# Cross-attention and int8-style FFN on one core: tokens laid out transposed outside the kernel, a levelled Wq, and another order on TensorE

## The reference

```python
def _attn_block(x, y):                       # x is layernorm(x)
    y_main, y_dca = y[:, :-16], y[:, -16:]
    kv_dca = y_dca @ Wkv_dca + bkv_dca       # keys and values of the 16 dca rows
    q = _ln(heads(x @ Wq + bq), qn_w, qn_b)  # 16 heads of 32, normalised per head
    k, v = ...                               # from y_main @ Wk + bk, y_main @ Wv + bv
    ctx = softmax(q k / sqrt(32)) v  +  softmax(q k_dca / sqrt(32)) v_dca
    return ctx @ Wo + bo
x = x + _attn_block(_layernorm(x), ctx_1024)
x = x + fake_quant(relu(fake_quant(_layernorm(x)) @ fake_quant(kernel) + bias))
```

## Time and profile before

| | |
|---|---|
| time, median of 3 runs | 368.29 us (367.71 to 371.18) |
| the profiled execution | 370.66 us, its span 368.8 us |
| PE busy | 319.3 us, 87% |
| DVE busy | 315.0 us, 85% |
| ACT busy | 222.5 us, 60% |
| POOL busy | 174.3 us, 47% |
| mean granted TensorE clock | 0.965 |

### The profile page before, as it was taken

One profiled execution on the slowest core, in us unless ns is written; L12 is line 12 of the kernel. 1 busy time (PEld: TensorE's weight loads), 2 busy tenths in 40 slices (PEclk: granted clock), 3 DMA queues, 4 the chain that ended last, 5 costly groups with the idle time before them and its releaser, 6 DMA issues.

```text
span 368.8 us, 7583 instructions
## 1 busy us (share of the span) xinstructions
PE 319.3 (87%) x2338; PEld 257.3 (70%) x2353; DVE 315.0 (85%) x804; ACT 222.5 (60%) x444; POOL 174.3 (47%) x261
## 2 busy tenths in 40 slices
PE   1498989799989999999898999999998999868732
PEld 0345657688877878787787888878787878566620
DVE  2987899799979899989898998989998999975664
ACT  3357886366666767676758585848584856552501
POOL 5201513327281828282828281828282837281620
PEclk9999899699999999999999999999999999998985
DMA  8870458507070909190909082828292616180002
GB/s 267 263 265 1 82 121 142 125 29 163 15 177 11 194 22 191 34 199 18 195 17 189 31 139 81 128 93 130 92 135 84 123 54 123 54 145 2 28 0 85
DMA packets 36451, 39.14 MB, mean 106 GB/s; under 512 B 8760, under 2 KB 27452, under 8 KB 36412
## 3 DMA queue, kind: packets, MB, share of 16 engines
q1 hardware_dynamic: 36044, 38.40, 48.2%
q10 hardware_dynamic: 368, 0.27, 0.3%
HBM read 17.15 MB, written 4.72 MB: 59 GB/s over the span
## 4 chain that ended last, share of the span: by engine, by line
PE 52%; DMA 9%; SPq 7%; issue 7%; DVE 3%; ACT 2%; POOL 0%; ACTq 0%; DVEq 0%
PE bank L1323 26%; SPq L372 7%; PE bank L1440 7%; DMA q_stack<-q_lo 7%; PE bank L1409 4%; PE bank L1596 4%; PE bank L1606 2%; PE bank L1420 2%; PE bank L1421 2%; PE bank L1463 2%; PE bank L1493 1%; DMA k_stack<-k_lo 1%; ACT k_hi L606 1%; PE bank L1498 1%; PE bank L1455 1%
## 5 line engine op out<-in xcount | busy, mean ns | idle before, releaser
L1440 PE MATMUL bank<-v_aug,prob_store 128*128 128x66 f32 x512 | 68.6, 278 | 3.4 <-ACT prob_store L744 3.4
L511 POOL TENSOR_TENSOR k_lo<-wkv_raw,k_hi 128x448 f16<-128x448 f32 x16 | 16.7, 1042 | 113.8 <-issue 105.9
L1440 PEld LDWEIGHTS bank<-v_aug,prob_store 128*128 128x128 f32 x512 | 64.4, 195 | 5.9 <-ACT prob_store L744 4.6
L1056 DVE TENSOR_REDUCE neg_max<-bank 128x4 f32<-128x448 f32 (+1 forms) x128 | 45.2, 416 | 9.9 <-PE bank L1409 9.9
L755 ACT ACTIVATE wkv_raw<-bank,affine 128x448 f32<-128x448 f32 (+1 forms) x32 | 22.4, 747 | 42.4 <-PE bank L1493 42.1
L744 ACT ACTIVATE prob_store<-bank,exp_scale 128x512 f32<-128x512 f32 x64 | 41.6, 677 | 4.9 <-PE bank L1421 4.8
L530 POOL TENSOR_TENSOR finals<-seg_out 128x128 f32<-128x128 f32 x64 | 34.4, 546 | 13.7 <-DVE seg_out L1069 13.4
L1420 PE MATMUL bank<-q_stack,k_stack 128*128 128x128 f16 x256 | 33.9, 220 | 1.9 <-ACT maxT L606 1.9
L1421 PE MATMUL bank<-maxT,sel 128*128 128x128 bf16 x256 | 33.7, 219 | 0.0
L1420 PEld LDWEIGHTS bank<-q_stack,k_stack 128*128 128x128 f16 x256 | 26.4, 104 | 6.1 <-issue 3.9
L1069 DVE TENSOR_TENSOR seg_out<-bank,rden 128x256 f32<-128x256 f32 x64 | 27.2, 424 | 3.8 <-POOL finals L530 1.7
(11 more groups left out here) (213 smaller groups left out, 876.9 us busy)
## 6 DMA issues: line engine op xcount, KB each, us to landing
x_in<-in_x SPq DMA_DIRECT2D x16, 256.0 KB, 4.9
q_stack<-q_hi SPq DMA_DIRECT2D x32, 128.0 KB, 3.7
q_stack<-q_lo SPq DMA_DIRECT2D x32, 128.0 KB, 4.6
k_stack<-k_hi SPq DMA_DIRECT2D x32, 128.0 KB, 3.3
k_stack<-k_lo SPq DMA_DIRECT2D x32, 128.0 KB, 4.3
out<-finals SPq DMA_DIRECT2D x16, 256.0 KB, 3.8
y_in<-in_ctx SPq DMA_DIRECT2D x16, 128.0 KB, 4.6
y_dcaT<-in_x SPq DMA_DIRECT2D x8, 256.0 KB, 4.3
```

The source lines that it names most:

```text
L1056: v.tensor_reduce(neg_max[:, HG * gr:HG * (gr + 1), seg], s4[:, :, lo:hi], AX.X, ALU.max, negate=True).then_inc(max_ready.sem, 1)
L1440: last = mm(bank[6 + gr % 2][:, VW * h:VW * (h + 1)], probs[:, gr % 2, h], v_aug[:, Bt.parity, HG * gr + h], start=True, stop=True)
```

## The change

Outside the kernel, numpy lays out: for each batch one array `xyT` of x transposed and the 112 main context rows transposed (128 partitions x 736 numbers); the dca rows transposed (`dcaT`); the six norm vectors as one row and, with the bias columns, as columns.

- **Tokens.** TensorE no longer transposes y, x or the dca rows, nor makes the columns. `xyT` of batch L comes with one DMA, behind `x_in`, the residual load and the load of the dca values; `high_context` and `high_stream` on ACT make `yT_hi`, `xT_hi` of batch L (from batch 2 on these stand first in ACT's step), `low_context` and `low_stream` on POOL make the low parts in place of `x_norm`. DVE loses both `low_part` calls for tokens.
- **Levelled Wq.** The raw x goes into the q product. The mean of Wq's columns over the 512 inputs is taken off in setup (`setup_sums` on TensorE: 4 full-precision matmuls; `level_queries` on DVE), which removes the mean of x; the reciprocal deviation is applied behind the product, in `biased_queries` (now one `scalar_tensor_tensor`).
- **TensorE's order in a full step:** k product of A, scores 2 and 3, output product, transposes of `k_t`, `q_t`, transpose of the maxima, first half of q, shifted 0 and 1, second half of q, weigh 0, shifted 2, weigh 1, shifted 3, weigh 2, weigh 3, transposes of `f_int`, v product of A, FFN product, scores 0 and 1, context transposes. Where there is no C yet, k stays behind the transposes of `q_t`.
- **ACT:** the copy of `maxT` goes ahead of `k_hi`; the square of q and the relu ahead of the copy of `f_intT`; the logarithm and exponential of the head norm (`heads`) and the copy of v go to the end of the step before. **DVE:** the head means and the Newton steps go to the end of the step before. **Setup:** one half of Wkv_dca is centred by POOL, its other half is loaded later; other loads are in another order.

```diff
             def step(L, A, N, Bt, C, D):
-                if L is not None and L.has(2):
-                    prev = L.back(2)
-                    sp.wait_ge(*xn_ready.of(prev))
-                    sp.dma_start(x_in[:, L.parity], x[L.index()]).then_inc(x_loaded.sem(L), 16)
-                    sp.wait_ge(*yT_ready.of(prev))
-                    sp.dma_start(y_in[:, L.parity], ctx[L.index()]).then_inc(y_loaded.sem(L), 16)
+                def tokens():
+                    if L is not None and L.has(2):
+                        prev = L.back(2)
+                        sp.wait_ge(*ln1_steps.of(prev, 2))
+                        sp.dma_start(x_in[:, L.parity], x[L.index()]).then_inc(x_loaded.sem(L), 16)
+                        for read in (xhi_ready, xlo_ready, yhi_ready, ylo_ready):
+                            sp.wait_ge(*read.of(prev))
+                        sp.dma_start(xy_in[:, L.parity], xyT[L.index()]).then_inc(xy_loaded.sem(L), 16)
+
+                if N is None or not N.has(2):
+                    tokens()
...
                     if N.has(2):
                         residual()
                         dca_values()
+                        tokens()
...
+                def low_stream(b):
+                    pool.wait_ge(*xy_loaded.of(b))
+                    low_tokens(b, xT_lo[:], xT_hi[:, b.parity], stream_in(b.parity), xhi_ready,
+                               q_ready.of(b.back(1)) if b.has(1) else None, xlo_ready)
...
+                def high_context(b):
+                    act.wait_ge(*((first_context.sem, 16) if b.first() else xy_loaded.of(b)))
+                    if b.has(2):
+                        act.wait_ge(*v_ready.of(b.back(2)))
+                    copy(flat(yT_hi[:, b.parity]), context_in(b.parity)).then_inc(yhi_ready.sem, 1)
...
+                if L is not None and L.has(2):
+                    high_context(L)
+                    high_stream(L)
                 if N is not None:
                     if N.first():
                         setup_dca(0)
                     normed(kT_ready, 6, MAIN, 2, k_n, kn_ready, klo_ready)
                     normed(qT_ready, 2, P, 0, q_n, qn_ready, qlo_ready)
+                if Bt is not None and not Bt.first():
+                    turned_maxima()
+                if N is not None:
                     high(k_hi, k_n, kn_ready, MAIN, kstack_in, khi_ready)
                     high(q_hi, q_n, qn_ready, P, qstack_in, qhi_ready)
...
+            def level_queries():
+                dve.wait_ge(wqsum_ready.sem, 1)
+                level = bank[0][:, :].unsqueeze(1).to_broadcast([P, XC // 2, D])
+                for half in range(2):
+                    part = slice(XC // 2 * half, XC // 2 * (half + 1))
+                    v.tensor_tensor(wq_raw[:, part], wq_raw[:, part], level, ALU.subtract).then_inc(wq_levelled.sem, 1)
...
+            def setup_sums():
+                pe.wait_ge(tiles_made.sem, 8)
+                for c in range(XC):
+                    pe.wait_ge(wq_centred.sem, 1 if c < XC // 2 else 2)
+                    last = mm(bank[0][:, :], per_token[:].to_broadcast([P, P]), wq_raw[:, c, :], start=c == 0, stop=c == XC - 1)
+                last.then_inc(wqsum_ready.sem, 1)
...
-                if A is not None:
-                    p = A.parity
-                    pe.wait_ge(*y_loaded.of(A))
...
-                    for c in range(XC):
-                        last = tr(bank[0][:, P * c:P * (c + 1)], x_norm[:, p, P * c:P * (c + 1)], ident[:])
-                    last.then_inc(xT_ready.sem, 1)
+                if A is not None and C is not None:
+                    key_product()
...
                 if Bt is not None:
                     weigh(2)
+                    weigh(3)
                 if C is not None:
                     pe.wait_ge(*fint_ready.of(C))
...
                     last.then_inc(fT_ready.sem, 1)
-                if Bt is not None:
-                    weigh(3)
+                if A is not None:
+                    if A.first():
+                        pe.wait_ge(wvlo_ready.sem, 2)
+                    pe.wait_ge(*kraw_ready.of(A))
+                    split_product(bank[3][0:MAIN, :], yT_hi[:, A.parity], yT_lo[:, A.parity], wv_hi, wv_lo, range(YC), MAIN
+                                  ).then_inc(v_ready.sem, 1)
```

More of the change, by code:

```diff
@@ L339, in _ @@
                      bias_parts[:, part])
+            sp.dma_start(x_in[:, 1], x[1]).then_inc(x_loaded.sems[1], 16)
+            sp.dma_start(xy_in[:, 1], xyT[1]).then_inc(xy_loaded.sems[1], 16)
             load(fk_in, fk_raw[:], chunked(ffn_kernel))
+            load(wdv_in, wd_raw[:, :, 1], chunked(Wkv_dca)[:, :, D:2 * D])
             load(wo_in, wo_raw[:], chunked(Wo))
@@ L433, in step @@
                         dca_values()
[L435 removed]
+            sp.wait_ge(tiles_made.sem, 8)
             run(sp, step)
@@ L554, in step @@
                         dca_columns(k_lo, kdca_lo)
-                        low(k_lo, k_n, k_hi, kn_ready, khi_ready, kstack_in, klo_ready, MAIN)
+                if N is not None and not N.first():
+                    low(k_lo, k_n, k_hi, kn_ready, khi_ready, kstack_in, klo_ready, MAIN)
                 centred()
@@ L596, in step @@
                     combine(3)
+                if L is not None and not L.first():
+                    low_stream(L)
             run(pool, step, {-2: setup_selected})
@@ L811, in step @@
                     setup_dca(1)
-                if L is not None and not L.second():
-                    token_statistics()
+                if L is not None and L.has(2):
+                    token_statistics(L)
                 if Bt is not None:
@@ L816, in step @@
                     expo(1)
+                if L is not None and L.second():
+                    high_context(L)
+                    high_stream(L)
                 if A is not None and not A.first():
@@ L827, in step @@
                     expo(3)
-                if C is not None:
-                    act.wait_ge(*fT_ready.of(C))
-                    if C.has(1):
-                        act.wait_ge(*ffn_ready.of(C.back(1)))
-                    copy(flat(f_intT[:]), bank[1][:, :].bitcast(BF16)[:, 0:P * XC]).then_inc(fintT_ready.sem, 1)
                 if A is not None:
@@ L837, in step @@
                     s.activation(q_sq, q_raw[:, A.parity], ACT.Square).then_inc(qsq_ready.sem, 1)
+                if D is not None and not final(D):
+                    relu()
+                if C is not None:
+                    act.wait_ge(*fT_ready.of(C))
+                    if C.has(1):
+                        act.wait_ge(*ffn_ready.of(C.back(1)))
+                    copy(flat(f_intT), bank[1][:, :].bitcast(BF16)[:, 0:P * XC]).then_inc(fintT_ready.sem, 1)
+                if A is not None:
+                    heads(A)
                 if N is not None and N.first():
-                    heads(A)
                     setup_wo()
@@ L843, in step @@
                     setup_selectors()
-                if D is not None and not final(D):
-                    act.wait_ge(*yrnd_ready.of(D))
-                    if D.has(1):
-                        act.wait_ge(*result_ready.of(D.back(1)))
-                    s.activation(f_u, f_yr, ACT.Relu, bias=minus_round[:, 0:1]).then_inc(u_ready.sem, 1)
+                if A is not None:
+                    values()
                 if Bt is not None and final(Bt):
@@ L1141, in head_products @@
                                     ).then_inc(qt_ready.sem, 1)
-                if N is not None and not N.second():
-                    head_means(N)
                 if D is not None and final(D):
```

358 lines of the change are left out of this document (178 added, 180 removed).

## The result

The changed kernel takes **389.19 us** (median of 4 runs, 387.65 to 391.34); the kernel before takes 368.63 beside it (367.71 to 371.18). The ratio is 1.053, 95% interval 1.047 to 1.058. The forecast was 375, the range 363 to 380. The profiled execution after has 387.65 us and a span of 385.8, that of before 370.66 and 368.8: 17.0 apart. The other 3.6 of the medians' difference is that the first of the two was the fastest of its runs (1.5 under the median) and the second 2.0 over its own.

The account below looks back on a forecast made before the run. Two nearly equal rings bound the step: PE's row (18.03) and the stack loads (18.64). Terms 1.2 + 3.1 + 0.8 - 0.7 + 2.6 = +7.0 on 368.3 gave 375 us, range 363 to 380.

Parts of the forecast that it names:

- K to the next S: Full step from the start of the k_t transposes (K) to the next start of scores 0 (S).
- wait of 1.28: Full step, PE ahead of the first q matmul: idle until ACT has read q_t from bank[2], 1.28 us per step.
- the likeliest case: Whole kernel slower, 371 to 379 us, chance 0.5.
- A: Rival, whole kernel: faster because the q wait is short and loads land in time, 358 to 365 us, chance 0.2.
- C: Rival, stall near batch 3's load: lower clock adds 4 us, giving 379; range 378 to 382, chance 0.1.
- K falls to S + 5.57 ... I see no new wait: Full step, scores 0 (S) to k_t transposes (K): six transposes, 0.65 us, come off with no new wait.
- POOL ... I cost it at 0: Full step: POOL's two two-input low-part passes, 1.27 us each, cost 0 given 7.24 us idle.
- (b): Start, batch 3's xyT load, the first through SP: ACT waits for it, +3.1 us, bounds 0 and +4.5.
- (c): Start, the step after batch 3's load: the second FFN half on DVE delays weigh 3, +0.8 us.
- (d): Start: batch 2's token transposes no longer stand in that first step, -0.7 us.
- (a): Start, Wq's setup chain: batch 0's k_t comes 1.2 us later, bounds -1 and +3.
- Tail: End of the row, where no A is left: nothing saved, 0.

Follow-up runs that it names:

- e5: Changed kernel with POOL's low_stream moved from the step's end to behind DVE's head products in the next step: 390.05 us.
- e11: Changed kernel with low_stream later from batch 3 on, batch 3's tokens issued early, relu behind the f_intT copy in steps without a new batch: 379.99 us.
- e3: Changed kernel with the q product of the full steps written to bank 0 instead of bank 2, so it need not wait for q_n: 389.75 us.
- e16: e11 with the q product in bank 0, so it need not wait for q_n: 380.23 us.
- e18: Changed kernel's layout with the engine orders of the kernel before, batch 3's tokens early, POOL's token low parts and token scale moved: 364.66 us, ratio 0.984.
- e4: Changed kernel with SP issuing batch 3's tokens ahead of its waits for the dca values: 385.04 us.
- e12: Changed kernel with the levelling of Wq (setup_sums and level_queries) left out: 390.28 us.
- e9: Kernel before with one unused two-operand POOL pass of 512 columns added per step from batch 3 on: 372.67 us, ratio 1.007.
- e8: Changed kernel with ACT's relu put back behind the f_intT copy: 398.80 us.

## Why the prediction was wrong

**What held.** K to the next S was forecast at 18.86 - 5.57 = 13.29 and measured 13.23; that this number came out is partly luck, as the step on the wait of 1.28 below shows. The wait at q was 1.08 (forecast 1.28), PE no longer waits for the stacks, and the load of batch 3 holds ACT for 4.2. The wait at weigh 3, for which 0.2 was taken, isn't there. The direction and the likeliest case were right, and A (faster because transposes vanish) did not come. C (the clock behind the stall near 60 us) didn't either: that stretch has 0.93 after and 0.91 before.

**Step "K falls to S + 5.57 ... I see no new wait"** failed. It measured 5.92, and 5.59 in e5 and e11, where GpSimd's pass doesn't hold DVE. Of the 0.65 of transposes 0.31 came off; the other 0.34 in each of 12 steps, **4 us**, is the collision.

**Step "POOL ... I cost it at 0"** is the same fault at its root. I weighed POOL's idle time (7.24 a step) and the price of its passes, and asked only who waits for their results. The pass was hidden on POOL and paid for on DVE. In the steps of the kernel before, the Newton passes ran where POOL was idle, and nothing shows; the one meeting at 57.74 in that trace I had not looked for. The rule of the Trainium skill, SBUF — State Buffer, section SBUF: two separate sides, speaks against this edit, and I had weighed only how fast GpSimd is.

**Step "wait of 1.28" as what the step costs** had about the right size and the wrong cause. By e3 and e16, taking it away gives nothing: weigh 2 still starts at K + 8.6, and PE waits for ACT on the way. What the changed order costs is read from the table: K to weigh 2 lost PE's k product (1.48) and got 0.1 shorter; weigh 2 to S got v (1.48) and, less the 0.6 of waiting for stacks, 0.9 longer. Work was moved out of a stretch in which PE waits anyway into one in which it doesn't. With the Newton passes' collisions gone on both sides the changed orders give 18.80 (e16) and the old ones 17.78 (e18). From weigh 2 to S that is 4.66 against 3.22, the length of the v product. But e16 and e18 differ in ACT's and DVE's orders too, so that PE's order alone makes this 1.0 is argued from the rows, not shown.

**Start**, forecast +4.4 up to batch 3, measured +7.3. Term (b), the load, was 3.1 and is 3.1 at batch 2 by e4 (1.7 at batch 3). Terms (c) and (d) were not measured apart. Term (a), Wq's chain, was +1.2 at batch 0, at most +3, and is +3.4. I costed the levelling alone; e12 shows a second chain beside it that ends only 0.8 earlier (the products start at 23.11 in place of 23.90). That is the centring of Wkv_dca, which had been put behind Wq's and onto POOL, ahead of products that q of batch 0 stands behind, and I did not follow that queue. I had named the high parts of batch 1 and the Newton passes ahead of the dca rows; behind q they come to 1.3 of the 1.7.

**Tail**, "0", measured +3.8, of which 1.7 to 2.7 is ACT's relu ahead of the `f_intT` copy and the rest goes with a lower clock. In a full step the relu's input has long been there; in the last two it has not. I had read the order in a full step alone.

The sum in the profiled pair: steps +5.9 where +2.6 was forecast, start +7.3 for +4.4, tail +3.8 for 0. The three misses, 3.3, 2.9 and 3.8, are the 10.0 between 7.0 and 17.0. The range failed since its upper end took in only terms that I had named.

## What to carry to other kernels

Before moving a pass to an engine with idle time, lay the two engines' timelines over each other and look for passes that will run at the same time; if the busier engine's total goes up while its instruction count goes down, compare the mean length of each small pass before and after. Ahead of the change, look in the old trace for a pass that is far longer than its like, and for what the other engine did beside it. A wait in the row of the busiest engine is not its cost: take it away (another buffer will do) and see whether it comes back further on in the row. Moving work pays by the stretch that it leaves and costs by the one that it enters, so read both, and read start and tail as steps of their own, where an order that is free in the steady state can put a wait in front of the last chain.

## What the runs showed of the hardware

- A DVE pass on 128x32 numbers with two SBUF operands takes 0.18 to 0.19 alone and 1.02 to 1.27 beside a POOL pass of 1.04 to 1.30 on SBUF operands, ending within 0.05 of it (1.02 in the kernel before, 1.05 in e9, 1.20 in the changed kernel, 1.20 and 1.27 in e8).
- The reverse, in e5: a POOL copy of 64 numbers a partition takes 0.24 alone and 1.95 beside two DVE passes of 1.08 and 1.09.
- A DVE pass with one operand in PSUM and one in SBUF keeps its 0.42 beside a POOL pass. A one-operand cast from SBUF to SBUF is held: in e18 the cast of the maxima takes 0.78 beside POOL's low part of the stream, and 0.18 in the changed kernel. DVE and then POOL in e18:

```profile
224.07 0.78 DVE L1242 CAST max_parts<-neg_max 128x32 bf16<-128x32 f32 x1
```

```profile
223.52 1.29 POOL L544 TENSOR_TENSOR xT_lo<-xy_in,xT_hi 128x512 fp32r<-128x512 f32 x1
```
